# Where the last feed-forward sums of blocks 13 and 14 are formed, in a fused token-mixing and feed-forward layer

## The reference, cut to what matters

```python
h = _L0_tok_ref(x, L0_tok_weight, L0_tok_extra)
h = h + _L0_attn_ref(_layernorm(h, axis=-1), L0_attn_W_act, L0_attn_W_val, L0_attn_W_rec)
h = h + _L0_ffn_ref(_layernorm(h, axis=-1), L0_ffn_weight, L0_ffn_rram_variation)

def _L0_ffn_ref(x, weight, rram_variation):
    x_q = ternary_quantize(x, TH_X, SC_X)      # 0.5, 0 or -0.5
    w_q = ternary_quantize(weight, TH_W, SC_W)
    w_rram = w_q + rram_variation
    return jnp.einsum('bsd,od->bso', x_q, w_rram)
```

## Time and profile before

| | us |
|---|---|
| median of 3 runs | 851.94 (851.32 to 852.45) |
| profiled execution | 852.92 |
| its span, from the first to the last instruction | 851.1 |
| TensorE busy in it | 797.8 (94%) |
| VectorE | 727.3 (85%) |
| ScalarE | 581.0 (68%) |
| GpSimd | 149.9 (18%) |

### The profile page before, as it was taken

How to read it: one execution, slowest core, us unless ns; L and a number is a source line. 1 busy time by engine, 2 the same in 40 slices (tenths; PEclk the granted TensorE clock), 3 DMA queues, 4 the chain that set the end, 5 groups by cost and what they waited for, 6 DMA issues and landing times.

```text
span 851.1 us, 12321 instructions
## 1 busy us (share of the span) xinstructions
PE 797.8 (94%) x4766; PEld 470.5 (55%) x4766; DVE 727.3 (85%) x1151; ACT 581.0 (68%) x582; POOL 149.9 (18%) x117
## 2 busy tenths in 40 slices
PE   1696987999999999999999999999999999999996
PEld 0453636456474746556474756647474655647442
DVE  6889689898989888888988988888988888876986
ACT  2478866778685867678586867768586767856471
POOL 5213300113120200202020110202020020000033
PEclk9898999999999999999999999999999999999999
DMA  8446421519081642909082391809655370802015
GB/s 303 99 141 157 94 55 38 99 47 212 3 193 30 129 94 84 140 6 211 7 167 57 106 118 59 164 1 163 60 130 94 89 134 15 161 0 75 0 27 171
DMA packets 152346, 83.74 MB, mean 98 GB/s; under 512 B 138352, under 2 KB 138480, under 8 KB 152288
## 3 DMA queue, kind: packets, MB, share of 16 engines
q1 hardware_dynamic: 145808, 63.04, 36.8%
q0 software_dynamic: 5392, 17.83, 8.9%
q10 hardware_dynamic: 1088, 2.10, 0.7%
HBM read 24.28 MB, written 16.78 MB: 48 GB/s over the span
## 4 chain that ended last, share of the span: by engine, by line
PE 71%; DVE 12%; ACT 6%; issue 3%; DMA 0%; POOL 0%; DVEq 0%; ACTq 0%
PE bank L356 23%; PE bank L393 22%; PE bank L422 15%; PE bank L436 10%; DVE chain L725 3%; DVE h L887 1%; DVE r L879 1%; DVE stats L893 1%; ACT x_hi L516 1%; ACT chain L653 1%; DVE stats L777 1%; DVE chain L827 1%; DVE chain L855 0%; DVE chain L846 0%; ACT r L544 0%
## 5 line engine op out<-in xcount | busy, mean ns | idle before, releaser
L422 PE MATMUL bank<-wval_hi,kv 128*128 128x512 f16 x512 | 156.4, 382 | 7.2 <-DVE kv L862 6.6
L356 PE MATMUL bank<-xT_hi,wact_hi 128*128 128x256 f16 x768 | 117.7, 277 | 10.1 <-ACT bank L523 4.2
L277 POOL DMA_INDIRECT h<-table,rows x64 | 93.6, 1463 | 171.3 <-DMA out<-h 131.3
L356 PE MATMUL bank<-xT_lo,wact_hi 128*128 128x256 f16 x768 | 118.1, 278 | 5.4 <-DMA xT_lo<-x_lo 5.4
L356 PE MATMUL bank<-xT_hi,wact_lo 128*128 128x256 f16 x768 | 117.5, 276 | 0.0
L393 PE MATMUL bank<-wrec_hi,xT_hi 128*128 128x512 f16 x384 | 99.4, 382 | 3.5 <-ACT bank L528 3.5
L436 PE MATMUL bank<-wffn_hi,qT 128*128 128x512 f16 x256 | 98.0, 383 | 4.1 <-DMA qT<-q 4.1
L393 PE MATMUL bank<-wrec_lo,xT_hi 128*128 128x512 f16 x384 | 99.3, 381 | 0.0
L393 PE MATMUL bank<-wrec_hi,xT_lo 128*128 128x512 f16 x384 | 98.5, 379 | 0.0
L436 PE MATMUL bank<-wffn_lo,qT 128*128 128x512 f16 x256 | 98.0, 383 | 0.0
L422 PE MATMUL bank<-wval_lo,kv 128*128 128x512 f16 x256 | 97.8, 382 | 0.0
(11 more groups left out here) (109 smaller groups left out, 1349.3 us busy)
## 6 DMA issues: line engine op xcount, KB each, us to landing
out<-h SPq DMA_DIRECT2D x15, 1024.0 KB, 5.6
xs<-xo SPq DMA_DIRECT2D x16, 448.0 KB, 3.5
chain<-w_act SPq DMA_DIRECT2D x4, 512.0 KB, 5.6
h<-w_rec ACTq DMA_DIRECT2D x4, 512.0 KB, 8.0
h<-table,rows POOLq DMA_INDIRECT x64, 6.1
kv<-w_val SPq DMA_DIRECT2D x1, 1024.0 KB, 5.7
r<-w_ffn SPq DMA_DIRECT2D x1, 1024.0 KB, 8.8
h<-w_var POOLq DMA_DIRECT2D x1, 1024.0 KB, 7.3
```

What stands on the lines that cost most here:

```text
L277: pool.indirect_dma_start(h[:, j % SLOTS, t, :], None, table, bass.IndirectOffsetOnAxis(ap=rows[:, TT * j + t:TT * j + t + 1], axis=0),).t ...
L356: ins = pe.matmul(dst.rearrange("p (s t) -> p s t", s=NSEQ), wact[a][:, kind, k, c * P:(c + 1) * P], xT[i % 2][b][:, kind, :, k, :], start ...
L422: ins = pe.matmul(bank[t + 4 * (j == LAST)][:, :], kv[a][:, k // 2, k % 2, t * P:(t + 1) * P], wval[b][:, k, :], start=(n == 0), stop=(n = ...
```

## The change

VectorE forms the final sums of blocks 13 and 14 itself, with the step that it uses for the other blocks: `final(LAST - 2, t)` right before the written-out loop of block 15, `final(LAST - 1, t)` right after it, ahead of `final(LAST, t)`. ScalarE's eight copies and GpSimd's eight sums are gone, with their two semaphores. The stores of the two blocks, and TensorE's wait before block 14's products, go by `s_fin`.

```diff
 (SyncE)
-                if j > LAST - 3:
-                    sp.wait_ge(s_finp, 4 * (j - LAST + 2) + 4)
-                else:
-                    sp.wait_ge(s_fin, 4 * j + 4)
+                sp.wait_ge(s_fin, 4 * j + 4)
...
-                sp.wait_ge(s_fin, 4 * (LAST - 2) + t + 1)
+                sp.wait_ge(s_fin, 4 * LAST + t + 1)
 (GpSimd)
-            def final_add(j):
-
-                for t in range(TT):
-                    rows_t = h[:, j % SLOTS, t, :]
-                    pool.wait_ge(s_evac, 4 * (j - LAST + 2) + t + 1)
-                    pool.tensor_tensor(rows_t, rows_t, spare(t), ALU.add).then_inc(s_finp, 1)
-
...
-                if t == 0:
-                    final_add(LAST - 2)
-            final_add(LAST - 1)
 (TensorE)
-                pe.wait_ge(s_evac, t + 1)
+                pe.wait_ge(s_fin, 4 * (LAST - 2) + t + 1)
                 ffn_product(LAST - 1, t)
 (ScalarE)
-            for j in (LAST - 2, LAST - 1):
-                for t in range(TT):
-                    act.wait_ge(s_fps, 4 * j + t + 1)
-                    if j == LAST - 1:
-                        act.wait_ge(s_finp, t + 1)
-                    act.activation(spare(t), bank[t][:, :], ACT.Identity, scale=unscale[:, FFN_W:FFN_W + 1])\
-                        .then_inc(s_evac, 1)
 (VectorE)
             for r in range(PAIRS):
                 last_kv_lo(r)
+            for t in range(TT):
+                final(LAST - 2, t)
             for t in range(TT + 2):
...
-            for t in range(TT):
-                final(LAST, t)
+            for j in (LAST - 1, LAST):
+                for t in range(TT):
+                    final(j, t)
```

More of the change, by code:

```diff
@@ L113, in tower_kernel @@
         sign = q[:, :, :].rearrange("p t d -> p (t d)")
-        def spare(t):
-            return (xo, xe)[t // 2][:, t % 2, :]
         def two_tap(nat):
@@ L174, in tower_kernel @@
         s_qT = [sem(f"s_qT{t}") for t in range(TT)]
-        s_evac, s_finp = sem("s_final_evacuated"), sem("s_final_pool")
         s_fps, s_fin, s_out = sem("s_ffn_product"), sem("s_final"), sem("s_stored")
```

## The result

The changed kernel took 844.70 us, the median of seven runs (843.64 to 847.05), and the kernel before, timed beside it, 849.59 (848.65 to 852.45, seven runs). The ratio is 0.9939, with a 95% interval of 0.9923 to 0.9955: about 0.6% less time, which is 5.2 us of 850; the two medians themselves are 4.9 apart. The forecast was 846.0 with a range from 845.2 to 848.6, so the median lies 0.5 us under the range, although the span of the profiled run is the 845.2 us forecast. The three runs of before that it started from all stood high, and their spread of 0.6 us was far too small for the range. And one term of the sum, the time from a store's last byte to the end, was too small, so the gain came out smaller than the forecast 5.9.

A forecast was written before the change was run, and what follows sets the result against it. VectorE's steps, lengthened 6.40 us beside GpSimd's additions, kept TensorE waiting for `qT`; TensorE's lowered clock was the other cost. With stores ending the span at 845.2 instead of 851.1, 5.9 us off 851.94 gave 846.0, range 845.2 to 848.6.

The forecast's parts named there:

- The long steps: VectorE in block 15: seven steps lengthened beside GpSimd's additions; without these its loop ends 6.40 us earlier.
- The powers: GpSimd's four powers for `std` stay and were counted as 0 us; rival that they block VectorE too, chance 0.10.
- Block 13's sums are covered: VectorE before block 15's first gate: four sums fit its 2.93 us standstill, cost nothing, 0.2 us to spare.
- TensorE goes through: TensorE's last 32 products run without waiting for `qT`, at full clock, ending at 841.8 against 847.87.
- the other cost, the clock: TensorE's last sixteen products: granted clock 0.85 of 2.4 GHz after the standstill, 0.33 us each against 0.216.
- Block 14's store: Store behind VectorE's loop: issued at 838.48 instead of 843.48, bytes moving at 384 GB/s from 839.50.
- The stores' end: End of span: 2.10 MB of stores end at 844.96, plus 0.25 us, giving 845.2.
- The base: Median of the kernel before, taken as 851.94 us; less 5.9 us this gave 846.0.

The follow-up runs named there:

- Without the cover: Changed kernel with block 13's four sums moved from ahead of block 15's first gate to ahead of the second: 849.04 us, ratio 0.9958 to the kernel before.
- before again: The kernel before, unedited, timed against itself and profiled a second time: 851.08 us, ratio 0.9993.
- The store in halves: Changed kernel with block 14's 1 MB store in two transfers, each behind its two sums: 846.12 us, ratio 0.9932 to the kernel before.
- the start ordered: GpSimd's large recurrent-weights addition waits for VectorE's first `x_lo`: in the changed kernel 844.86 us, ratio 0.9917; in the kernel before 850.04 us, 0.9983.
- The two halves of the change: Only block 13's or only block 14's sums by VectorE, the other block's as before: 848.05 us, ratio 0.9962, and 848.84 us, 0.9961.

## Why the prediction was right, and where it was wrong

The mechanism was right. What put the measured median under the stated range was the base and the spread that the range was built on, and what made the gain smaller than forecast was one term of the stores. The figures are from the first gate's start, which takes the start's levels out.

- **The long steps are GpSimd's doing.** Shown by taking the additions away and by putting idle ones back. Leaving the loop was forecast at 835.73 - 820.29 = 15.44 and came at 15.44: the 6.40 us were right.
- **The powers cost nothing.** Right by the rows above: no step of VectorE is longer beside them.
- **Block 13's sums are covered.** Forecast to take 2.72 us and to end 0.2 before the gate; they took 2.72 and left 0.30. Without the cover they cost 2.5, forecast 2.7.
- **TensorE goes through.** End forecast at 21.5, measured 841.40 - 819.92 = 21.48. (Tile 3's `ternary` was put at 835.75; 842.21 - 6.40 is 835.81, without effect.) What the prediction calls the other cost, the clock, was no fixed part of the kernel before: before again has the same standstill at the 2.4 GHz level. It decides 0.3 us of the end, and so whether the gain by the traces is 5.5 or 5.2.
- **Block 14's store** was forecast at 18.19 and issued at 18.18; the rate forecast at 384 GB/s was 381. The 358 GB/s of the Trainium skill's page SBUF — State Buffer ("A bandwidth-pool intuition that's wrong") would have been too low here.
- **The stores' end, mis-sized.** This is the term of the sum that failed: "2.10 MB at 384 GB/s end at 844.96, plus 0.25". I took 0.25 us from the last byte to the end of the span, because I had closed the window of the lone tile at 850.85. It measured 0.8 after (844.40 to 845.20). In before, too, the bytes end earlier than I read, at about 850.35: the lone tile's 187 GB/s in the earlier trace rows is a mean over a stretch that ran on behind its last byte. Bytes flowed 0.80 us after the issue, not 1.02, which gave 0.2 back. So gate to end is 25.28 instead of 24.91, and the gain 5.2 to 5.5 us instead of 5.9. The store in halves shows that this is where the end is set. By itself this term makes the time longer than forecast, so it is not what put the median under the range.
- **The base, not a constant.** This step put the measured median outside the range. "851.94 - 5.9 = 846.0 for the median" took the three runs shown as the kernel's level, and the lower end of the range allowed only "the spread of the runs shown, 0.6". Of the seven runs of before in the comparison these three are the highest (851.32 to 852.45), and the other four lie between 848.65 and 849.59: a spread of 3.8 us and a median of 849.59. From that base the forecast gain would have given 843.7, and the measured 5.2 gives 844.4, against 844.70 measured. The two profiles of before show two orders at the start, 3.1 us apart from `x_lo` on, and 3.6 apart at the first gate; which order the unprofiled runs had is not known. With the start ordered, the change's gain is 5.2 us. That the changed kernel's profile has exactly my span of 845.2 is luck: its start was 0.37 us earlier and its tail 0.37 longer, and both first profiles happened to have GpSimd's addition first.

What stays open is the rest of the spread, some 3 us in kernels with an ordered start.

## What to carry to other kernels

An engine that is only 18% busy can still cost the critical one: look for one operation and shape with two durations on the critical engine, and for what runs beside the long ones. Before elementwise work is handed to GpSimd to spare VectorE, look at which of VectorE's steps will run beside it: here eight additions lengthened the steps with two inputs in SBUF, and `below`, by 6.4 us in all. Doing the sums in one step each on VectorE, half of them in a gap where it stood still, was 5.2 us cheaper. And before a forecast is tied to a median, the trace should be asked whether two engines race for something early on, because a few runs may all have fallen on one side; a range needs the spread of more than three runs.

## What the runs showed that I had not expected

- The level of the runs is set in the first 45 us, in part by whether GpSimd's 4.53 us addition or VectorE's 1.23 us `x_lo` starts first: in the first profile of before 0.25 us lie between their starts. The profiles of either order are 1.4 to 3.1 us apart, and forcing the order gave 1.3 to 1.6.
- From the last byte of a store to the end of the span some 0.8 us pass in which the DMA engines show no traffic, in both kernels.
- The same standstill of 2.4 us for `qT` was followed by the lower level of TensorE's clock in one profile of the kernel before and not in another.
- The two halves of the change add up (2.4 + 2.8 against 5.2), although each leaves GpSimd busy in the other half.
